# Attention scores in both orders, probabilities written already transposed, and the causal mask as a product in either kind

## The chip, the cores and the metric

One Trainium2 chip, one of its cores. The metric is device time in microseconds from the program's start to its end. TensorE (PE) multiplies, VectorE (DVE) and ScalarE (ACT) empty its banks (PSUM, eight banks of 128 x 512 fp32), GpSimd (POOL) and SyncE (SP) mostly issue transfers here.

## The reference

x is 8 x 512 x 256. Each batch goes through a layer, attention and a feed-forward layer; then a mixture of experts follows for all 4096 tokens.

```python
y = einsum('bnh,boh->bno', x, weight[itok]) + bias[itok]            # layer chosen by batch
Q, K, V = heads(y @ W_Q), heads(y @ W_K), heads(y @ W_V)             # 16 heads of 16
scores = einsum('bhqd,bhkd->bhqk', Q, K) / 4 + causal                # -inf above the diagonal
out = einsum('bhqk,bhkd->bhqd', softmax(scores), V)                  # then reshaped
x = x + out @ W_o
hidden = relu(x @ wi.T + low-rank terms)                             # 1024 wide
h = hidden @ wo.T + low-rank terms
gate = softmax(h @ gate_w + gate_b); top 2 of 8 experts
x = x + sum over the top 2 of gate * expert(h)                       # three layers, gelu
```

## The kernel before, in words

**Stages.** The main stage runs nine rounds (`Round`, b from 0 to 8). Round b computes the attention of batch b and, in the same instruction streams, the feed-forward part of batch b - 1; round 0 has only the first, round 8 only the second. Then come the routing of tokens to experts and 71 tiles of 128 gathered tokens through the experts' three layers. The experts' weights are split into a high and a low part during the rounds: GpSimd loads a piece, ScalarE rounds it (`cast`, L990), GpSimd subtracts (L1516) and writes both to memory (L1521), eight pieces in each attending round.

**Precision.** Most products are of fp32r operands; where more is needed an operand stands as high part plus low part, and a product is three. Transposes and the values times probabilities take fp32.

**One attending round.** `opening` lists the projections q, k, v, the parts of q and k brought into place per pair of heads (`qs`, `ks`, with the constant `sel`), the previous batch's output projection `x1t` and its first hidden tiles. Each head's q and k lie in a strip of 64 rows, its 16 numbers as high and low parts in four groups of 16 rows, so that one product of height 64 gives the score in the precision wanted. Then 35 steps follow (`STEPS`). `units_at(step)` tells for each step:
- two units `s` (a unit is one query tile i of 128 rows and one head; there are 64, sorted by query tile, so that widths are 128, then 256, 384, 512 keys). For each, TensorE adds the causal mask of the last 128 keys as a bf16 product (`mask_b`, `id_b`) and then the score, in a bank of the ring [0, 1, 2]. VectorE takes the negated maximum of each row (L1276), ScalarE the exponential with that as bias per row and with its row sums (L1092), into `probs`;
- two units `t`, one step later: TensorE transposes the 128 x 128 blocks of `probs` (L831, ring [4, 5]); VectorE (L1290) or ScalarE (L1100, `on_act`) copies them to `probs_t`;
- in every second step four units `pv`: values times transposed probabilities, four heads in four groups of 32 columns of the array, fp32, into bank 6;
- at the end of a query tile the reciprocals of the sums (L1301, L1303), their transposes `rt` (L839), and the scaling of the result into `ot_sb` (L1282);
- one piece of filler: the feed-forward of the previous batch or the layer ahead of the next batch (`FILLERS`, ring [3, 7]).

The order on each engine is that of the code; a bank has one semaphore counting its fillings and one counting its emptyings (`filled`, `drained`, `vacant`). A wait on TensorE holds back all that follows it. All products have L665 in the profile (`mm`), and are told apart by their operands.

The lines that the change touches are those of the steps: TensorE's `turn`, ScalarE's `turn` with L1092 and L1100, VectorE's `turn` with L1276, L1290, L1301 and L1303, `psum_plan`, `opening`, and SyncE's loads of the residual (`x_res`) and of the low-rank weights.

## Time and profile before

| what | us |
|---|---|
| median of 3 runs (lowest, highest) | 1510.2 (1505.05, 1514.26) |
| the profiled execution | 1507.66 |
| its span on the core | 1506.1 |
| TensorE busy in the span | 1359.4 |
| weight loads of TensorE (overlap it) | 1053.1 |
| VectorE busy | 875.0 |
| ScalarE busy | 767.0 |
| GpSimd busy | 420.0 |

Mean granted clock of TensorE: 0.955 of full speed. Busy times of pipelined instructions overlap and hold latencies, so the time that one group costs is read from its start to the start of the next. In a row of the timeline, "x2" after a shape means two instructions of the same kind, and the bracket at the end is idle time of the engine before it with what ended it. "2 matmuls" of an fp32 product may be two instructions for one product.

### The profile page before, as it was taken

The numbers are of one execution on the slowest core, as the hardware profiler recorded it, in microseconds if no ns is written. First come the engines' busy times: TensorE is split into PE (matmuls) and PEld (weight loads), VectorE is DVE, ScalarE is ACT, GpSimd is POOL, SyncE is SP. The second block draws the span as 40 slices with busy tenths as digits, with TensorE's granted clock in tenths as the row PEclk, the third lists the DMA queues.
The fourth block names the chain that finished last, engine by engine and source line by source line (L and its number), as shares of the span: only waits on it lengthen the run. The fifth ranks groups of instructions, "written<-read, shape, count | busy, mean of one in ns | idle before, by whom it ended". The sixth has DMA issues, their size and how long they took to land.

```text
span 1506.1 us, 32247 instructions
## 1 busy us (share of the span) xinstructions
PE 1359.4 (90%) x10297; PEld 1053.1 (70%) x10298; DVE 875.0 (58%) x1945; ACT 767.0 (51%) x2003; POOL 420.0 (28%) x553
## 2 busy tenths in 40 slices
PE   5989999999989989999999988249899999999997
PEld 3556766766766766766766757238788888888886
DVE  3765665665665665665666662645455555555554
ACT  4776676665666665675666651013233333333332
POOL 2212211221221211211212210133344444444442
PEclk9799999999999999999999999559999999999999
DMA  6112222222222222222222220652624223342221
GB/s 221 64 66 97 76 82 98 78 96 82 78 95 83 77 81 93 77 86 98 78 80 77 79 72 29 271 225 36 247 42 145 42 42 88 101 148 40 38 40 13
DMA packets 50642, 137.85 MB, mean 92 GB/s; under 512 B 10514, under 2 KB 29586, under 8 KB 48882
## 3 DMA queue, kind: packets, MB, share of 16 engines
q0 software_dynamic: 28992, 68.35, 16.9%
q1 hardware_dynamic: 21554, 68.18, 12.3%
q8 instruction: 65, 1.06, 0.3%
q14 instruction: 31, 0.25, 0.1%
HBM read 86.03 MB, written 51.38 MB: 91 GB/s over the span
## 4 chain that ended last, share of the span: by engine, by line
PE 81%; DVE 5%; ACT 4%; issue 4%; DMA 4%; POOL 1%; SPq 0%; POOLq 0%; DVEq 0%; ACTq 0%
PE bank L665 66%; PE bank L831 9%; PE bank L924 4%; ACT probs L1092 3%; DVE nmax L1276 2%; PE bank L916 1%; DMA xg<-hrows,gid 1%; DMA w_rest<-in_w_all 1%; DMA wsplit<-w_rest 1%; POOL hit_v L1536 0%; PE bank L839 0%; ACT w_high L990 0%; DVE probs_t L1290 0%; POOL w_rest L1516 0%; PE bank L779 0%
## 5 line engine op out<-in xcount | busy, mean ns | idle before, releaser
L1092 ACT ACTIVATE probs<-bank,nmax 128x512 f32<-128x512 f32 (+3 forms) x512 | 266.0, 525 | 164.4 <-DVE nmax L1276 163.0
L1276 DVE TENSOR_REDUCE nmax<-bank 128x1 f32<-128x512 f32 (+3 forms) x512 | 227.3, 486 | 201.7 <-PE bank L665 201.3
L1128 ACT ACTIVATE g<-z 128x512 f32<-128x512 f32 x142 | 89.8, 632 | 281.3 <-DVE z L1466 270.0
L831 PE MATMUL bank<-id_f,probs 128*128 128x128 f32 x1280 | 203.1, 290 | 0.4 <-ACT probs_t L1100 0.4
L1516 POOL TENSOR_TENSOR w_rest<-w_rest,w_high 128x512 f32<-128x512 f32 x64 | 81.4, 1271 | 425.5 <-ACT w_high L990 425.5
L665 PE MATMUL bank<-wst,g1t_high 128*128 x568 | 186.0, 409 | 0.9 <-DVE g1t_low L1454 0.9
L831 PEld LDWEIGHTS bank<-id_f,probs 128*128 128x128 f32 x1280 | 137.8, 143 | 45.0 <-issue 24.2
L1558 POOL DMA_INDIRECT out<-y_sb,sid x71 | 114.3, 1610 | 149.7 <-PE bank L916 67.1
L1290 DVE COPY probs_t<-bank 128x128 f32<-128x128 f32 (+3 forms) x320 | 140.1, 454 | 12.6 <-PE bank L831 12.6
L1466 DVE TENSOR_TENSOR z<-bank,b_sb 128x512 f32<-128x512 f32 x142 | 98.2, 692 | 74.3 <-PE bank L665 63.2
L665 PEld LDWEIGHTS bank<-wst,g1t_high 128*128 128x128 f32 x568 | 102.5, 190 | 20.8 <-issue 1.1
L665 PE MATMUL bank<-wst,g1t_low 128*128 x284 | 113.4, 399 | 0.0
L665 PE MATMUL bank<-wst,g2t_high 128*128 x568 | 107.7, 289 | 1.5 <-DVE g2t_low L1454 1.5
L665 PE MATMUL bank<-k_sb,q_sb 64*128 64x512 f32 (+3 forms) x512 | 107.8, 418 | 0.0
L665 PE MATMUL bank<-mask_b,id_b 128*128 128x128 bf16 x512 | 84.6, 228 | 21.2 <-ACT probs L1092 17.4
L1092 ACT ACTIVATION_READ_ACCUMULATOR probs<-bank,nmax 128x1 f32 x512 | 101.3, 198 | 0.0
L665 PE MATMUL bank<-probs_t,v_sb 128*32 128x128 f32 x2560 | 98.4, 281 | 0.0
L665 PE MATMUL bank<-wst,xgt_high 128*128 x284 | 96.9, 423 | 1.3 <-DVE xgt_low L1454 1.3
L1513 POOL DMA_DIRECT2D w_rest<-in_w_all x64 | 35.0, 546 | 216.4 <-DMA wsplit<-w_rest 216.4
L1548 POOL DMA_INDIRECT xg<-hrows,gid x71 | 76.2, 1073 | 63.8 <-POOL gid L1545 56.8
L665 PEld LDWEIGHTS bank<-probs_t,v_sb 128*32 128x32 f32 x2560 | 62.9, 110 | 41.9 <-issue 28.4
L1100 ACT COPY probs_t<-bank 128x384 f32<-128x384 f32 (+3 forms) x192 | 88.3, 460 | 3.1 <-PE bank L831 2.9
(213 smaller groups left out, 2879.2 us busy)
## 6 DMA issues: line engine op xcount, KB each, us to landing
wst<-wsplit SPq DMA_DIRECT2D x8, 4096.0 KB, 12.6
w_rest<-in_w_all POOLq DMA_DIRECT2D x64, 256.0 KB, 3.1
wsplit<-w_high POOLq DMA_DIRECT2D x64, 256.0 KB, 2.3
wsplit<-w_rest POOLq DMA_DIRECT2D x64, 256.0 KB, 2.6
hrows<-h_sb SPq DMA_DIRECT2D x8, 528.0 KB, 3.0
x_in<-in_xT SPq DMA_DIRECT2D x8, 512.0 KB, 3.5
wb_raw<-in_lora_wb SPq DMA_DIRECT2D x8, 512.0 KB, 3.5
x_res<-in_xT SPq DMA_DIRECT2D x8, 512.0 KB, 4.5
```

Source lines behind the costliest of these rows:

```text
L665: return nc.tensor.matmul(*a, **k)
L831: ins = nc.tensor.transpose(at(n, rd)[:, kb * P:(kb + 1) * P], probs[:, t % 4, kb * P:(kb + 1) * P], id_f[:, :])
L924: ins = nc.tensor.transpose(bank[bt][:, k * P:(k + 1) * P], g[:, k * P:(k + 1) * P], id_f[:, :])
L1092: taken(nc.scalar.activation(probs[:, s % 4, 0:(i + 1) * P], at(n, rd)[:, 0:(i + 1) * P], ACT.Exp, bias=nmax[:, s % 8:s % 8 + 1], accum_ou ...
L1100: taken(nc.scalar.copy(probs_t[:, t % PT_SLOTS, 0:w], at(n, rd)[:, 0:w]), n, rd)
L1128: nc.scalar.activation(g[:, :], z[:, :], ACT.Gelu).then_inc(s_g, 1)
L1276: V.tensor_reduce(nmax[:, s % 8:s % 8 + 1], at(n, rd)[:, 0:(s // HEADS + 1) * P], AX.X, ALU.max, negate=True).then_inc(s_max, 1)
L1290: taken(V.tensor_copy(probs_t[:, t % PT_SLOTS, 0:w], at(n, rd)[:, 0:w]), n, rd)
L1466: V.tensor_tensor(z[:, :], bank[bl][:, :], bias[:, bass.ds(e, 1), :].rearrange("p o n -> p (o n)"), ALU.add).then_inc(s_z, 1)
L1516: nc.gpsimd.tensor_tensor(w_rest[:, :], w_rest[:, :], w_high[:, :].bitcast(F32), ALU.subtract).then_inc(s_wlow, 1)
L1548: nc.gpsimd.indirect_dma_start(xg[:, buffer, :], None, hrows, bass.IndirectOffsetOnAxis(ap=gid[:, 0:1], axis=0), bounds_check=B * S - 1, o ...
L1558: nc.gpsimd.indirect_dma_start(out_rows, bass.IndirectOffsetOnAxis(ap=sid[:, 0:1], axis=0), y_sb[:, buffer, :], None, bounds_check=B * S - ...
```

## The change

- The order of the steps is now by pairs of heads. A pair has three chunks of scores: query tile 3 (512 keys), tiles 2 and 0 in one bank (384 + 128), tile 1 (256). Each chunk takes a bank for either head. They serve only for the row maxima on VectorE (L1276).
- The negated maxima of a pair are split into high and low parts (`m_parts` in `mm_sb`), brought by four products per pair with an identity (`id_r`) into rows `M_ROW`, `M_ROW + 1` of either head's strip, and copied by ScalarE into `q_sb`. k's strip has ones there (`marks_sb[:, 0]`), added when `ks` is emptied; `sel` leaves these rows free.
- Five steps after the first kind, the scores are computed a second time with keys as rows and queries as columns (`st`, ring [4, 5]), with the mask product in the other order; they now hold the maximum's subtraction. ScalarE takes the exponential straight into `probs_t`, without bias and without sums. The transposes, their copies, `probs` and the sums' reads are gone. 64 scores and 64 masks a round become 128 and 128.
- `v_sb` has 16 columns of ones beside each head's 16 of values, so the value product gives the sums too. One group of four heads (`quad`) runs over four key blocks of 512, 384, 256 and 128 columns in one bank: 16 products in place of 40. The result is divided between `ot_sb` and `sums` by masks (`marks_sb[:, 1]`, `[:, 2]`), on ScalarE for even quads and on VectorE for odd ones.
- Twice in a round `sums` is transposed (`nn`, four transposes), its reciprocals are taken and spread (`rrep`), transposed back (`nr`, four) and multiplied into `ot_sb`. Before, the reciprocals were transposed per query tile, two transposes each.
- 34 steps in place of 35, with none, one or two fillers each (`FILL_COUNTS`); `low_o` in four pieces. The residual is loaded into `x1t` in place of `x_res`, after the transposes of x1 are emptied. The low-rank loads wait for the output's transfer as well. GpSimd's part of the stage (split of the experts' weights) stays; its memset fills the ones instead of zeros.

The diff, cut to its core:

```diff
+PAIRS = HEADS // 2
+QUADS = PAIRS // 2
+SCORE_CHUNKS = ((3,), (2, 0), (1,))
+KEY_CHUNKS = ((0,), (3, 1), (2,))
+CHUNKS = len(SCORE_CHUNKS)
+PT_AT = {0: 0, 3: S, 1: S + P, 2: 2 * S}
+PT_COLS = 2 * S + 2 * P
+M_ROW = 32
+MM_COLS = P + 2 * TB
+M_LAG, ST_LAG, PV_LAG, NORM_LAG, SCALE_LAG = 4, 5, 12, 20, 21
+STEPS = NORM_LAG + 2 + 6 * (QUADS - 2)
...
+def work_at(step):
+
+
+    return (chunk_at(step), chunk_at(step - ST_LAG), every(step - M_LAG, CHUNKS, PAIRS),
+            every(step - PV_LAG, 2 * CHUNKS, QUADS), every(step - NORM_LAG, 4 * CHUNKS, KD),
+            every(step - SCALE_LAG, 4 * CHUNKS, KD))
...
+FILL_COUNTS = [2] * 5 + [1] * 7 + [0] + [1] * 5 + [0, 1, 0, 1, 1, 1, 0] + [2] * 5 + [0, 1, 0, 1]
...
-    rings = {"linear": [0, 1, 2, 3, 7, 4, 5, PV_BANK], "score": [0, 1, 2], "filler": [3, 7], "t": [4, 5],
+    rings = {"linear": [4, 5, PV_BANK, 0, 1, 2, 3, 7], "score": [0, 1, 2], "filler": [3, 7], "st": [4, 5],
...
-            probs_t = sb("probs_t", [P, PT_SLOTS, S], F32, attn)
+            v_sb = sb("v_sb", [P, TB, KD, 4, 3, DH], F32, attn)
...
+        def m_parts(part):
+
+            return (mm_sb[:, 0:P].rearrange("p (h c) -> p h c", h=2)[:, :, M_ROW:M_ROW + 2 * TB]
+                    .rearrange("p h (i s) -> p h i s", s=2)[:, :, :, part])
...
-                        pe.wait_ge(free[PV_BANK], rd.start(PV_BANK, 1))
+                        drained(pe, ("nr", KD - 1), Round(p))
...
+                    if score is not None:
+                        g, u = score
+                        if u == 0:
+                            drained(pe, ("qs", g), rd)
+                            drained(pe, ("ks", g), rd)
+                        for half in range(2):
+                            n = ("s", g, u, half)
+                            vacant(pe, n, rd)
+                            for c, (_, cols) in enumerate(query_tiles(u)):
+                                mm(at(n, rd)[:, cols.stop - P:cols.stop], id_b[:, :], mask_b[:, :], start=(c == 0),
+                                   stop=False, skip_group_check=True)
+                    if late is not None:
+                        g, u = late
+                        if u == 0:
+                            drained(pe, ("m", g), rd)
+                        for half in range(2):
+                            n = ("st", g, u, half)
+                            vacant(pe, n, rd)
+                            for c, (_, cols) in enumerate(key_tiles(u)):
+                                mm(at(n, rd)[:, cols.start:cols.start + P], mask_b[:, :], id_b[:, :], start=(c == 0),
+                                   stop=False, skip_group_check=True)
+                    if score is not None:
+                        g, u = score
+                        for c, (i, cols) in enumerate(query_tiles(u)):
+                            for half in range(2):
+                                n, r = ("s", g, u, half), STRIP * half
+                                ins = mm(at(n, rd)[:, cols], q_sb[r:r + STRIP, g, i * P:(i + 1) * P],
+                                         k_sb[r:r + STRIP, g, 0:(i + 1) * P], start=False, stop=True,
+                                         skip_group_check=True)
+                                if c == len(SCORE_CHUNKS[u]) - 1:
+                                    done(ins, n, rd)
+                    if late is not None:
+                        g, u = late
+                        for c, (kb, cols) in enumerate(key_tiles(u)):
+                            for half in range(2):
+                                n, r = ("st", g, u, half), STRIP * half
+                                ins = mm(at(n, rd)[:, cols], k_sb[r:r + STRIP, g, kb * P:(kb + 1) * P],
+                                         q_sb[r:r + STRIP, g, kb * P:S], start=False, stop=True, skip_group_check=True)
+                                if c == len(KEY_CHUNKS[u]) - 1:
+                                    done(ins, n, rd)
+                    if m is not None:
+                        n = ("m", m)
+                        vacant(pe, n, rd)
+                        pe.wait_ge(s_msplit, b * PAIRS + m + 1)
+                        for i in range(TB):
+                            ins = mm(at(n, rd)[:, i * P:(i + 1) * P], mm_sb[:, 2 * i:2 * i + P], id_r[:, :],
+                                     start=True, stop=True)
                         done(ins, n, rd)
-                    if rt is not None:
-                        n = ("rt", rt)
-                        pe.wait_ge(s_rrep, b * TB + (rt + 1))
+                    if norm is not None:
+                        n = ("nn", norm)
+                        vacant(pe, n, rd, [("pv", 2 * norm + 1)])
+                        for i in range(TB):
+                            ins = nc.tensor.transpose(at(n, rd)[:, i * P:(i + 1) * P], sums[:, i * P:(i + 1) * P], id_f[:, :])
+                        done(ins, n, rd)
...
-                        for k in range(KD):
-                            ins = nc.tensor.transpose(at(n, rd)[:, k * P:(k + 1) * P],
-                                                      rrep[:, k * P:(k + 1) * P], id_f[:, :])
+                        pe.wait_ge(s_rrep, b * KD + scale + 1)
+                        for i in range(TB):
+                            ins = nc.tensor.transpose(at(n, rd)[:, i * P:(i + 1) * P], rrep[:, i * P:(i + 1) * P], id_f[:, :])
                         done(ins, n, rd)
-                    if n_fill is not None:
...
-                            done(ins, n, rd)
+                    if quad is not None:
+                        n = ("pv", quad)
+                        vacant(pe, n, rd, [("v", t2) for t2 in range(TB // 2)] if quad == 0 else ())
+                        drained(pe, ("st", 2 * quad + 1, CHUNKS - 1, 1), rd)
+                        for kb in range(TB):
+                            for c in range(4):
+                                h = 4 * quad + c
+                                values = v_sb[:, kb, quad // 2, c, quad % 2:quad % 2 + 2, :]
+                                first = PT_AT[kb]
+                                ins = mm(at(n, rd)[PART * c:PART * (c + 1), kb * P:S],
+                                         values.rearrange("p a d -> p (a d)"),
+                                         probs_t[:, h % PT_SLOTS, first:first + S - kb * P],
+                                         start=(kb == 0), stop=(kb == TB - 1))
+                        done(ins, n, rd)
...
+                    _, late, m, quad, _, _ = work_at(step)
+                    if late is not None:
+                        g, u = late
+                        if u == 0 and g >= 3:
+                            filled(act, ("pv", (g - 3) // 2), rd)
+                        for half in range(2):
+                            n = ("st", g, u, half)
+                            width = key_tiles_width[u]
+                            filled(act, n, rd)
+                            taken(nc.scalar.activation(probs_t[:, (2 * g + half) % PT_SLOTS, S * u:S * u + width],
+                                                       at(n, rd)[:, 0:width], ACT.Exp), n, rd)
+                    if m is not None:
+                        n = ("m", m)
+                        filled(act, n, rd)
+                        for half in range(2):
+                            rows = slice(STRIP * half + M_ROW, STRIP * half + M_ROW + 2)
+                            ins = nc.scalar.copy(q_sb[rows, m, :], at(n, rd)[rows, :])
+                        taken(ins, n, rd)
+                    for n_fill, piece in rd.fillers(step):
+                        take(rd, n_fill, piece)
+                    if quad is not None and quad % 2 == 0:
+                        n = ("pv", quad)
+                        if quad:
+                            filled(act, ("nn", quad // 2 - 1), rd)
+                        filled(act, n, rd)
+                        nc.scalar.activation(ot_sb[:, quad // 2, :], at(n, rd)[:, :], ACT.Identity, scale=marks_sb[:, 1:2])
...
-                    ins = V.tensor_copy((q_sb if what == "qs" else k_sb)[:, m, :], at(n, rd)[:, :])
+                    ins = V.tensor_copy(q_sb[:, m, :], at(n, rd)[:, :])
+                elif what == "ks" and m % 2 == 1:
+                    filled(dve, n, rd)
+                    ins = V.tensor_scalar(k_sb[:, m, :], at(n, rd)[:, :], marks_sb[:, 0:1], None, ALU.add)
...
+                            for i, cols in query_tiles(u):
+                                ins = V.tensor_reduce(nmax[:, g % 2, half, i:i + 1], at(n, rd)[:, cols], AX.X, ALU.max,
+                                                      negate=True)
+                            taken(ins, n, rd)
+                        if u == CHUNKS - 1:
+                            drained(dve, ("s", g, u, 1), rd)
+                            if g > 0:
+                                filled(dve, ("m", g - 1), rd)
+                            V.tensor_copy(m_parts(0), nmax[:, g % 2, :, :]).then_inc(s_mhigh, 1)
+                            dve.wait_ge(s_mhigh, b * PAIRS + g + 1)
+                            V.tensor_tensor(m_parts(1), nmax[:, g % 2, :, :], m_parts(0).bitcast(F32), ALU.subtract
+                                            ).then_inc(s_msplit, 1)
                     if norm is not None:
-                        n = ("pv", norm)
-                        drained(dve, ("rt", norm), rd)
+                        n = ("nn", norm)
...
-            nc.gpsimd.memset(v_sb[:, :, :, :, :].rearrange("p t h a d -> p (t h a d)"), 0.0).then_inc(s_vzero, 1)
+            nc.gpsimd.memset(v_sb[:, :, :, :, 1, :].rearrange("p t k c d -> p (t k c) d"), 1.0).then_inc(s_vzero, 1)
...
         "sel": _np.stack([_np.tile(_np.kron(_np.eye(2), _np.kron(rows, _np.eye(DH))), (4, 1))
-                          for rows in ([[1, 0, 1, 0]], [[0, 1, 0, 1]], [[1, 1, 0, 0]], [[0, 0, 1, 1]])],
+                          for rows in ([[1, 0, 0, 1]], [[0, 1, 0, 0]], [[1, 1, 0, 0]], [[0, 0, 0, 1]])],
                          axis=1).astype(_np.float32),
+        "marks": _np.stack([(iota % STRIP // 2 == M_ROW // 2), (iota % PART < DH), (iota % PART >= DH)],
+                           axis=1).astype(_np.float32),
```

## Rows read from the trace of the kernel before

**Rows 1.** The page: busy times of the span, and the chain that ended last.

```profile
PE 1359.4 (90%) x10297; PEld 1053.1 (70%) x10298; DVE 875.0 (58%) x1945; ACT 767.0 (51%) x2003; POOL 420.0 (28%) x553
...
PE 81%; DVE 5%; ACT 4%; issue 4%; DMA 4%; POOL 1%; SPq 0%; POOLq 0%; DVEq 0%; ACTq 0%
```

**Rows 2.** Table by stretch: four of nine rounds. Bounds, length, busy times, clock, DMA, GB/s.

```profile
17.65:111.77 94.12, 79.50 (x705) 51.37 (x705) 63.66 (x143) 66.78 (x197) 21.75 (x31) 0.85 0.24 85
221.23:331.98 110.75, 103.94 (x921) 75.80 (x921) 70.05 (x161) 71.81 (x204) 23.32 (x32) 1.00 0.26 87
445.06:560.10 115.04, 107.24 (x920) 77.92 (x921) 70.03 (x161) 71.84 (x204) 23.33 (x32) 0.97 0.25 84
891.00:950.00 59.00, 40.35 (x216) 32.63 (x215) 17.82 (x42) 9.00 (x16) 0.00 (x0) 0.85 0.18 64
```

**Rows 3.** Timeline, PE: a round's first mask and the next round's first product. Start, length.

```profile
246.42 0.28 PE L665 MATMUL bank<-mask_b,id_b 128*128 128x128 bf16 x2
...
331.98 0.47 PE L665 MATMUL bank<-cond_high,wq_high 128*128 128x512 f32 x1 [1.56 <-issue]
```

**Rows 4.** Timeline, PE: the groups of one late step of the same round.

```profile
311.18 1.08 PE L665 MATMUL bank<-probs_t,v_sb 128*32 128x128 f32 x32
312.20 0.29 PE L665 MATMUL bank<-mask_b,id_b 128*128 128x128 bf16 x2
312.41 0.50 PE L665 MATMUL bank<-k_sb,q_sb 64*128 64x512 f32 x2
312.84 1.09 PE L831 MATMUL bank<-id_f,probs 128*128 128x128 f32 x8
313.77 0.60 PE L779 MATMUL bank<-id_f,h_sb 128*128 128x128 f32 x4
```

**Rows 5.** Timeline, PE: scores over 128 keys, their transposes, a filler.

```profile
250.53 0.33 PE L665 MATMUL bank<-k_sb,q_sb 64*128 64x128 f32 x2
250.78 0.44 PE L831 MATMUL bank<-id_f,probs 128*128 128x128 f32 x2
250.98 0.48 PE L665 MATMUL bank<-x_high,wi_high 128*128 128x512 f32 x1
...
251.76 0.28 PE L665 MATMUL bank<-mask_b,id_b 128*128 128x128 bf16 x2
```

**Rows 6.** Timeline, PE: the gate's products, reciprocals, next layer.

```profile
326.42 1.85 PE L665 MATMUL bank<-gw_sb,ht_sb 128*128 128x8 f32 x16
328.13 0.41 PE L839 MATMUL bank<-id_f,rrep 128*128 128x128 f32 x2
328.38 1.02 PE L665 MATMUL bank<-x_in,wc_sb 128*128 128x512 f32 x2
```

**Rows 7.** Groups by line, shapes apart: busy us, mean ns, idle before.

```profile
L831 PE MATMUL bank<-id_f,probs 128*128 128x128 f32 x1280 | 203.1, 290 | 0.4 <-ACT probs_t L1100 0.4
...
L1092 ACT ACTIVATE probs<-bank,nmax 128x512 f32<-128x512 f32 x128 | 87.0, 686 | 46.3 <-DVE nmax L1276 46.3
...
L1276 DVE TENSOR_REDUCE nmax<-bank 128x1 f32<-128x512 f32 x128 | 82.4, 686 | 56.9 <-PE bank L665 56.8
...
L1290 DVE COPY probs_t<-bank 128x512 f32<-128x512 f32 x64 | 43.6, 682 | 12.6 <-PE bank L831 12.6
...
L1100 ACT COPY probs_t<-bank 128x512 f32<-128x512 f32 x64 | 37.5, 586 | 3.1 <-PE bank L831 2.9
```

**Rows 8.** Timeline, ACT and PE: a mask that waited for an exponential.

```profile
360.95 0.19 ACT L1092 ACTIVATION_READ_ACCUMULATOR probs<-bank,nmax 128x1 f32 x1
...
361.19 0.23 PE L665 MATMUL bank<-mask_b,id_b 128*128 128x128 bf16 x1 [0.75 <-ACT probs L1092]
```

**Rows 9.** Timeline, ACT and DVE: casts over 32 and 96 rows, a low part.

```profile
325.38 1.04 ACT L1059 CAST wb_top<-wb_raw 32x1024 fp32r<-32x1024 f32 x1
...
327.24 1.04 ACT L1059 CAST wb<-wb_raw 96x1024 fp32r<-96x1024 f32 x1
...
329.06 1.22 DVE L1180 TENSOR_TENSOR wb<-wb_raw,wb_top 32x1024 fp32r<-32x1024 f32 x1
```

More of the change, by code:

```diff
@@ L59 @@
 W_PIECES = W_ALL // W_PIECE
-W_OPENING = (0, 10)
-W_STEPS = (2, 8, 14, 19, 23, 28)
 W_SLOTS = 3
@@ L1076, in turn @@
                     take(rd, n)
-                    if b is not None and rd.opening.index(n) in W_OPENING:
-                        cast(b, W_OPENING.index(rd.opening.index(n)))
+                    if b is not None and n in CASTS_AFTER:
+                        cast(b, CASTS_AFTER[n])
                 for step in range(STEPS):
-                    n_fill, piece = rd.filler(step)
                     if b is None:
-                        if n_fill is not None:
+                        for n_fill, piece in rd.fillers(step):
@@ L1103, in turn @@
+                    if step in CAST_STEPS:
+                        cast(b, CAST_STEPS[step])
                     if step in LORA_STEPS:
@@ L1292, in turn @@
+                    for n_fill, piece in rd.fillers(step - 1) if step > 0 else ():
                         take(rd, n_fill, piece)
```

308 lines of the change are left out of this document (136 added, 172 removed).

## The prediction

> **What bounds the kernel now.** I read the page's shares and the chain first [rows 1]: TensorE is busy for 90% of the span and carries 81% of the chain that ended last, so what counts is the time between the starts of TensorE's groups. Then the table by stage [rows 2]: the attention stage consists of nine rounds, of which eight attend; they lie between 17.65 and 891 us, and the span ends at 1506.1 us, so over 40% of the time (the last round, routing, the experts) is not touched. Then one attending round in order of time, that from 221.23 to 331.98 us: its steps run from the first causal mask at 246.42 to the next round's first matmul at 331.98, which comes after 1.56 us of idle time [rows 3]. That is 85.6 us of steps and 25.2 us of opening. The change leaves the opening's products as they are, so everything happens in the 85.6 us.
>
> **TensorE's attention work before, by start to start.** Two masks take 0.21 us and two scores over 512 keys 0.43 [rows 4]; over 128 keys the two scores take 0.25 [rows 5]. The two scores of a pair use different rows of the array and run side by side, so a pair costs about 0.06 per 128 keys and some 0.20 for starting. A round has 32 pairs, eight of each width: 8 x (0.25 + 0.31 + 0.37 + 0.43) + 32 x 0.21 = 17.6. Transposes: two take 0.20 [rows 5], eight take 0.93 [rows 4]; a round has 16 heads x 10 blocks = 160, eight rounds make the 1280 of the table [rows 7]: 17.4. Values times probabilities: four heads over four key blocks take 1.02 [rows 4]; the 32 instructions are 4 x 0.213 of streaming and 0.17 of start; 40 x 0.213 + 16 x 0.17 = 11.2. Four times two transposes of the reciprocals at 0.25 [rows 6] are 1.0. Together 47.2; the other 38.4 of the 85.6 are the previous batch's feed-forward pieces (I make them 31) and some 7 of stalls.
>
> **After, on TensorE, per round.**
> - Removed: the 160 transposes, -17.4.
> - Scores of both kinds: 128 masks at 0.053 (half of the 0.10 by which two masks exceed one start) are 6.8. The same columns twice are 160 blocks x 0.06 = 9.6. They come in 29 steps, each with one change into masks and one into half-height tiles: 29 x (0.11 + 0.19) = 8.7. The 35 pairs that follow another pair in their step need no new start. No row shows one such pair behind another. Bounds: nothing more than the columns, as between the four key blocks of the value products [rows 4], or the full 0.20 again [rows 5]. I take 0.05, near the value products, since these too change weights every instruction without leaving their tiling: 1.8 (0 to 7). Sum 26.9 against 17.6: +9.3.
> - The maxima as rows: 8 x 4 products of 128 columns. Sixteen weight loads with only eight columns each take 1.71 [rows 6], 0.107 each, so a 128-column product with new weights costs about that: 8 x (0.43 + 0.1) = +4.2.
> - Value products: the same 40 blocks, now 4 starts in place of 16: 9.2, -2.0.
> - Normalisation: 16 transposes in place of 8, in four groups: 2.1, +1.1.
>
> Net -4.8, bounds -7 and +1.
>
> **Stalls.** The transposed scores own two banks, and a step needs both free. So each step is a loop: ScalarE ends its second exponential; 0.05 later TensorE masks (361.19 against the end of the first operation at 361.14 [rows 8]); 0.17 later it scores; ScalarE starts 0.04 after the last pair ends. An exponential over 512 columns costs 0.686 with a pointer bias, a copy without one 0.586 [rows 7]. The new one has no pointer bias, so the copy is the nearer row; I take 0.59, and 1.09 for two overlapping ones.
>
> The Trainium skill (ScalarE: Activation LUTs, What ACT_TABLE_LOAD costs) says that a pointer operand adds about 93 ns to an ACTIVATE. By this rule the new exponential is the cheap one; if it were wrong, each 512-wide step would be 0.2 longer, about 3 us in a round. No row before shows an exponential of that width without bias.
>
> The steps repeat in threes. With 128+384 columns: 0.05 + 0.17 + 0.37 of scores + 0.52 for the last pair + 1.09 = 2.20. With 256: 0.93 to ScalarE, 0.65 for both, and then ScalarE copies the maxima into two rows of q at either half. A cast of 32 rows takes 1.04, as one of 96 does [rows 9], so height doesn't help, and two copies of 512 columns are 1.09; the next step's masks wait for them: 2.74. With 512: 2.02. Three steps are 6.96. TensorE's own work in them is 3.14 + 0.5 of maxima + 3 feed-forward pieces of 0.78 (250.98 to 251.76 [rows 5]) = 6.0, so it idles 1 us in 7. Steps 5 to 23 are six times 6.96, one of 2.0, and two with value products, each 1.2 over its loop: 46.2. Steps 0 to 4 have no transposed scores: scores 3.5, two pieces each 7.4, first maxima 0.5: 11.4. Steps 24 to 33: 3.1, 2.7, 2.3, 2.75, 1.95, 1.4, 2.3, 1.75 (the gate [rows 6]), 1.85 and 0.55; in the 1.85 TensorE waits some 1.3 for VectorE's reciprocals and their spreading. Sum 20.65. Together 78.3, against 85.6 before: -7.3. Of this 4.8 is work and 2.5 stalls, among them the 1.56 [rows 3], since the next batch's projections now end four steps before the round does.
>
> **What is free.** The copies of transposed probabilities leave both engines (0.586 and 0.682 for 512 columns [rows 7]) and the sums' reads leave ScalarE (0.19 [rows 8]), but neither engine was the bound: they gain only slack. It covers the new small work: VectorE per three steps has six maxima (0.686 for 512 columns [rows 7]; 3.6 in all), 0.5 for splitting the maxima and 0.3 of copies, in 7 us. The product of the maxima is issued two steps after they exist; TensorE's wait for it therefore costs nothing, and behind it would stand the step's feed-forward piece. At the round's end the last scale waits on VectorE behind the gate's work and a low part of 1.22 [rows 9]; TensorE meanwhile has the reciprocals' transposes and the first q and k, 3.3, against VectorE's 2.8. If that cover fails, the output projection is late by the difference. The residual, now loaded into the tile where it is added, is requested after step 4 and needed a round later. The expert adapters' loads start after step 26 and are needed 7 us later; the GpSimd chain (casts five or six steps apart, at some 2.3 each, so 12 us) keeps its place. Two key casts gain a pointer bias: 0.1 each, hidden.
>
> **Sum.** Seven rounds x 7 = -49. The first round has no feed-forward pieces: its loops are as long, so -6 by the same count, but it ran at a mean clock of 0.85 [rows 2], and TensorE will be idle for more of it, which I charge 5. So -50 on the profiled execution's 1507.7: 1457.7. The median lies 2.5 above that execution: 1460.
>
> **Rivals.**
> - A, forecast: -4 to -11 per round, 1425 to 1480. Chance 0.55.
> - B, following pairs pay a full start (35 x 0.15 = 5.3): -2 per round, 1495. For it: pairs of 64-row weights have been seen only alone. Chance 0.14.
> - E, loops hide better and TensorE's work alone counts (42 + 31 = 73): -12 per round, 1415. Chance 0.12.
> - D, slower: two banks are too few. The round trip decides once a step of 5 to 23 is 0.38 longer than I count (7.3 / 19), for instance if exponentials don't overlap (0.1 more), ScalarE wakes late (0.2), and the row copies come a further 0.6 late in every third step. At 0.75 longer: +7 per round, 1560 at worst, 1530 in the middle. Against it: the latencies are read from rows. Chance 0.12. The Trainium skill (TensorEngine Tiling (Array Packing), PSUM Bottleneck) warns that tiling speeds up TensorE but not the emptying of PSUM, which may become the bottleneck; this is the mechanism by which it would speak against the change. The trace before does not decide it: its scores had three banks and the transposes two.
> - C, slower by the clock. The round at clock 0.97 took 115.0 us against 110.8 at 1.00 with the same instructions [rows 2]. If the new idle time drew the clock to its lower level (1.2 GHz) for half of steps 5 to 23, their 38 us of TensorE work would double for that half, less the slack: +8 per round, 1570. It decides from about a quarter of the stretch on. Against it: TensorE stays some 85% busy there. Chance 0.07.
>
> Faster by over 0.5% takes A but 0.02, E, and 0.08 of B: 0.73. Within 0.5%: 0.08. Slower: D and C, 0.19. (0.5%, some 7.5 us, is about what a measurement of this kernel can tell from no change.) The range leaves out C, most of D and the lower half of E: 1415 to 1512.
>
> **What would show it.** Right: rounds of about 103 us; no transposes of probabilities; loops of 2.0, 2.2 and 2.7; exponentials at 0.59; idle time before the transposed masks, released by ScalarE; clock near 0.97. Wrong: a following pair over 0.2 (B), idle time over 1 us in every step with ScalarE idle too (D), low clock inside rounds (C).

## The result, and the profile after

| kernel | median us | ratio to before, 95% interval |
|---|---|---|
| before | 1513.2 (5 runs) | 1 |
| after | 1502.4 (5 runs) | 0.9942 (0.9914 to 0.9971) |

The changed kernel is 0.6% faster; its profiled execution took 1502.0 us with a span of 1500.4. The sign was right, the size a fifth of what was forecast: 1460 us with a range up to 1512. The spans differ by 5.7 us, where the forecast had 50.

The page of after: busy times, the clock in 40 slices of the span (9 is 90% or more of full speed), the chain.

```profile
PE 1331.8 (89%) x8825; PEld 999.2 (67%) x8826; DVE 802.8 (54%) x1753; ACT 684.5 (46%) x1301; POOL 418.3 (28%) x553
...
PEclk9569999999999999999999979559999999999998
...
PE 76%; ACT 11%; DVE 7%; DMA 3%; issue 3%; POOL 1%; SPq 0%; POOLq 0%; ACTq 0%; DVEq 0%
```

Against [rows 1], TensorE has 27.6 us less busy time, VectorE 72 and ScalarE 83, and the span hardly moved. TensorE's share of the chain fell from 81% to 76%, ScalarE's rose from 4% to 11%. In the clock row the second and third slice (37 to 112 us) stand out, which are the first round; the one at the 26th and 27th lies behind the attending rounds, and before has it too (its row is 9799..., with one low slice in the first round).

The table by stretch of after: the first and the fourth round (bounds, length, busy times of PE, PEld, DVE, ACT, POOL, clock, DMA share, GB/s).

```profile
17.01:124.78 107.77, 84.86 (x521) 47.74 (x521) 52.91 (x117) 57.30 (x112) 22.88 (x31) 0.71 0.21 81
341.42:450.08 108.66, 100.18 (x739) 69.33 (x737) 60.89 (x136) 61.30 (x116) 23.30 (x32) 0.99 0.25 88
```

The first round grew from 94.1 to 107.8 us, its mean clock fell from 0.85 [rows 2] to 0.71. The six full rounds after it take 108.7 on average ((776.74 - 124.78) / 6), against (785.51 - 111.77) / 6 = 112.3 before. The eighth has no next layer to start; up to the first product of its output projection it grew from 105.0 (890.55 - 785.51) to 108.4 (885.10 - 776.74). TensorE's last groups there, of before:

```profile
890.55 5.33 PE L665 MATMUL bank<-ot_sb,wo_sb 128*128 128x512 f32 x8 [1.46 <-DVE ot_sb L1282]
```

and of after:

```profile
880.48 1.09 PE L891 MATMUL bank<-id_f,sums 128*128 128x128 f32 x4 [1.55 <-DVE sums L1352]
882.58 1.08 PE L898 MATMUL bank<-id_f,rrep 128*128 128x128 f32 x4 [1.01 <-DVE rrep L1379]
885.10 6.25 PE L688 MATMUL bank<-ot_sb,wo_sb 128*128 128x512 f32 x8 [1.43 <-DVE ot_sb L1385]
```

The fourth round of after by stage: opening, steps 0 to 4, 5 to 23, 24 to 33.

```profile
341.42:366.34 24.92, 24.13 (x123) 16.96 (x121) 16.41 (x27) 14.04 (x27) 6.37 (x9) 0.95 0.38 128
366.34:380.63 14.29, 11.96 (x69) 8.32 (x69) 9.60 (x21) 5.24 (x9) 2.37 (x3) 1.00 0.08 33
380.63:427.56 46.93, 44.37 (x389) 31.66 (x386) 28.06 (x73) 28.61 (x57) 9.27 (x13) 1.00 0.24 81
427.56:450.08 22.52, 19.72 (x164) 12.39 (x162) 6.82 (x16) 13.41 (x24) 5.29 (x7) 1.00 0.27 96
```

The forecast for these was 25.2, 11.4, 46.2 and 20.65. The long middle came within 2%; the ends are where the time was lost.

The middle of that round, from ScalarE's and then TensorE's order of time.

```profile
401.29 0.66 ACT L1156 ACTIVATE probs_t<-bank 128x256 f32<-128x256 f32 x2
401.97 1.17 ACT L1163 CAST q_sb<-bank 2x512 fp32r<-2x512 f32 x2
404.11 1.08 ACT L1156 ACTIVATE probs_t<-bank 128x512 f32<-128x512 f32 x2 [0.98 <-PE bank L688]
...
403.19 0.28 PE L688 MATMUL bank<-id_b,mask_b 128*128 128x128 bf16 x2 [0.48 <-ACT q_sb L1163]
403.41 0.39 PE L688 MATMUL bank<-k_sb,q_sb 64*128 64x256 f32 x2
403.63 0.40 PE L688 MATMUL bank<-q_sb,k_sb 64*128 64x512 f32 x2
...
404.91 0.64 PE L688 MATMUL bank<-id_b,mask_b 128*128 128x128 bf16 x4
405.47 0.50 PE L688 MATMUL bank<-k_sb,q_sb 64*128 64x512 f32 x2
405.81 0.45 PE L688 MATMUL bank<-q_sb,k_sb 64*128 64x128 f32 x4
406.19 0.39 PE L688 MATMUL bank<-wf_high,hid_high 128*128 128x256 f32 x1
...
410.21 0.29 PE L688 MATMUL bank<-id_b,mask_b 128*128 128x128 bf16 x2 [0.36 <-ACT q_sb L1163]
```

The loop is what the prediction described. ScalarE's two row copies end at 403.14; the masks of the transposed scores start at 403.19, 0.05 later; scores 0.22 behind them; ScalarE starts at 404.11. Three steps, from 403.19 to 410.21, take 7.02 us; the count was 6.96. The pair of 512 columns of first scores takes 0.34 us and the two pairs of transposed scores behind it (128 and 384 columns) 0.38 together (rows 405.47, 405.81 and 406.19); by the prediction's prices a full start for each would have made it 0.44 and 0.64. So a pair behind a pair needs no full start: rival B is out. Rival D needed steps 0.38 longer than counted; these are 0.02 longer.

Groups of after by line, shapes apart (busy us, mean ns, then idle before them and its releasers).

```profile
L688 PE MATMUL bank<-id_b,mask_b 128*128 128x128 bf16 x512 | 73.0, 228 | 34.7 <-ACT q_sb L1163 26.5 <-ACT probs_t L1156 6.4
...
L1156 ACT ACTIVATE probs_t<-bank 128x512 f32<-128x512 f32 x256 | 139.0, 595 | 113.3 <-PE bank L688 113.3
...
L1163 ACT CAST q_sb<-bank 2x512 fp32r<-2x512 f32 x128 | 73.8, 577 | 8.3 <-PE bank L688 6.3
```

Exponentials of 512 columns are 0.595 us, not 0.686 [rows 7], 0.09 less without the pointer bias. The Trainium skill (ScalarE: Activation LUTs, What ACT_TABLE_LOAD costs) has 93 ns for a pointer operand, and the traces agree: 0.595 us here, 0.684 with the bias put back in `exp_bias`, further down. The copies of two rows cost 0.577 each, as full ones do. TensorE's idle time before the second kind of masks is 34.7 us in all, 26.5 of it for these copies.

The start of the steps in the fourth round, TensorE only.

```profile
366.34 0.22 PE L688 MATMUL bank<-mask_b,id_b 128*128 128x128 bf16 x1
367.83 0.23 PE L688 MATMUL bank<-mask_b,id_b 128*128 128x128 bf16 x1 [1.28 <-DVE hid_low L1287]
...
380.14 0.66 PE L819 MATMUL bank<-id_f,x1t 128*128 128x128 f32 x4 [1.05 <-DVE hid_low L1287]
```

The end of that round and the first products of the next.

```profile
434.69 0.29 PE L688 MATMUL bank<-id_b,mask_b 128*128 128x128 bf16 x2 [1.10 <-ACT q_sb L1163]
...
446.06 1.95 PE L688 MATMUL bank<-gw_sb,ht_sb 128*128 128x8 f32 x16
447.99 0.63 PE L891 MATMUL bank<-id_f,sums 128*128 128x128 f32 x4
449.63 0.80 PE L898 MATMUL bank<-id_f,rrep 128*128 128x128 f32 x4 [1.01 <-DVE rrep L1379]
450.08 0.78 PE L688 MATMUL bank<-cond_high,wq_high 128*128 128x512 f32 x1
450.65 0.63 PE L688 MATMUL bank<-cond_low,wq_high 128*128 128x512 f32 x1
```

Here are three waits that the forecast missed: 1.28 and 1.05 us for VectorE's low part of hidden tiles, and 1.10 for the row copies, which the forecast had in its loops but not as late as here. The fourth, 1.01 for the reciprocals, was in it at 1.3. What was not in it is what follows that one: the first q products start 0.57 and then 0.43 apart (450.08, 450.65), where before they were 0.31 and then 0.23 apart. TensorE is at its lower level, 1.2 GHz (granted clock 0.50 from 450.08 to 453.00), right after a stretch with a wait of 1.01 us, the 16 products of eight columns of the gate, and transposes. Five of the seven round ends in after have such a fall of the clock, all seven have the wait; so the wait alone does not decide it.

### The profile page after: what moved, and what is told of

Same layout as the page of the kernel before. It is cut to its first block, busy times and chain, and to the rows that moved or that the text cites. A ratio compares the mean times of both kernels' runs of the same rounds, so it can differ in the third digit from the quotient of the medians.

```text
span 1500.4 us, 27946 instructions
## 1 busy us (share of the span) xinstructions
PE 1331.8 (89%) x8825; PEld 999.2 (67%) x8826; DVE 802.8 (54%) x1753; ACT 684.5 (46%) x1301; POOL 418.3 (28%) x553
## 4 chain that ended last, share of the span: by engine, by line
PE 76%; ACT 11%; DVE 7%; DMA 3%; issue 3%; POOL 1%; SPq 0%; POOLq 0%; ACTq 0%; DVEq 0%
PE bank L688 69%; PE bank L978 4%; ACT probs_t L1156 4%; ACT q_sb L1163 4%; DVE nmax L1360 2%; PE bank L970 1%; DMA xg<-hrows,gid 1%; ACT ot_sb L1172 1%; DMA w_rest<-in_w_all 1%; PE bank L898 1%; ACT sums L1173 1%; DVE hid_low L1287 1%; DMA wsplit<-w_rest 1%; DVE ot_sb L1350 0%; ACT w_high L1044 0%
## 5 line engine op out<-in xcount | busy, mean ns | idle before, releaser
L1156 ACT ACTIVATE probs_t<-bank 128x512 f32<-128x512 f32 (+1 forms) x384 | 181.1, 524 | 166.7 <-PE bank L688 166.7
L688 PE MATMUL bank<-wst,g2t_high 128*128 x568 | 108.4, 291 | 1.5 <-DVE g2t_low L1544 1.5
L688 PE MATMUL bank<-id_b,mask_b 128*128 128x128 bf16 x512 | 73.0, 228 | 34.7 <-ACT q_sb L1163 26.5
L688 PE MATMUL bank<-k_sb,q_sb 64*128 64x512 f32 (+3 forms) x512 | 93.2, 402 | 0.0
L688 PE MATMUL bank<-mask_b,id_b 128*128 128x128 bf16 x512 | 72.4, 230 | 19.1 <-DVE nmax L1360 9.2
L978 PE MATMUL bank<-id_f,g 128*128 128x128 f32 x568 | 85.8, 274 | 2.4 <-ACT g L1194 2.4
L688 PEld LDWEIGHTS bank<-wst,g2t_high 128*128 128x128 f32 x568 | 86.5, 190 | 1.8 <-issue 1.7
L688 PE MATMUL bank<-q_sb,k_sb 64*128 64x512 f32 (+3 forms) x512 | 82.5, 360 | 0.0
L688 PE MATMUL bank<-probs_t,v_sb 128*32 128x512 f32 (+3 forms) x1024 | 80.6, 458 | 0.0
L688 PE MATMUL bank<-wf_high,hid_high 128*128 128x256 f32 x256 | 80.1, 313 | 0.0
L688 PE MATMUL bank<-wst,g2t_low 128*128 x284 | 79.2, 279 | 0.0
## 6 DMA issues: line engine op xcount, KB each, us to landing
wst<-wsplit SPq DMA_DIRECT2D x8, 4096.0 KB, 12.5
```

The costliest lines, as they stand in the source:

```text
L688: return nc.tensor.matmul(*a, **k)
L978: ins = nc.tensor.transpose(bank[bt][:, k * P:(k + 1) * P], g[:, k * P:(k + 1) * P], id_f[:, :])
L1156: taken(nc.scalar.activation(probs_t[:, (2 * g + half) % PT_SLOTS, S * u:S * u + width], at(n, rd)[:, 0:width], ACT.Exp), n, rd)
```

## Experiments

Each ratio is to the kernel before; after's is 0.9942 with 1502.4 us. The products that some of them add write into a bank whose contents are not read before it is overwritten, so they change only the time. The kernel before was run again beside each group of experiments, with medians of 1509.7 to 1511.7 us against 1513.2 beside after: a difference to after below some 3 us says little.

### first_round_full: the first round's gaps filled

```diff
+                    if p is None and step < 27:
...
+                        for _ in range(3 * FILL_COUNTS[step]):
+                            mm(bank[3][:, :], wq_high[:, 0, 0:P], cond_high[:, 0, :], start=True, stop=True)
```

> The changed kernel, with idle TensorE time of the first round filled: in its steps 0 to 26, three fp32r products of 512 columns into a free bank wherever a later round has a feed-forward piece (their result is overwritten). Nothing else changes, the output stays the reference's. Theory CLOCK: the first round took 107.8 us against 94.1 before because TensorE, with gaps at every step and no feed-forward work, stayed at the lower clock (mean 0.71). With the gaps filled the clock rises early and the first round falls to about 92 us; the whole to 1488. Rival WORK: the round is slow because its chain of ScalarE and VectorE is longer; then it stays at 105 to 110 us or gets longer by the added products, whole 1500 to 1510.

Measured: 1491.8 us, ratio 0.9868 (0.9840 to 0.9896), 10.6 less than after. Its first round, in the table by stretch:

```profile
16.82:112.10 95.28, 85.16 (x611) 53.69 (x611) 52.84 (x117) 57.31 (x112) 22.90 (x31) 0.98 0.25 93
```

95.3 us in place of 107.8, at a clock of 0.98 in place of 0.71, with 90 products more (521 to 611). More work in 12.5 us less time, while VectorE and ScalarE are as busy as in after (52.8 and 57.3 us): the clock is what changed. That the added products cost something at full clock, so that the round stopped at 95 and not at 92, is likely but not shown. Of the 12.5 us the second round gave back 0.8 (108.6 in place of 107.8) and the eighth 1.5 (109.9 in place of 108.4).

### before_first_round_full: the same for the kernel before

```diff
+                        for _ in range(3):
+                            mm(bank[3][:, :], wq_high[:, 0, 0:P], cond_high[:, 0, :], start=True, stop=True)
```

> The kernel before, with the same three products added in steps 0 to 26 of its first round. Theory CLOCK: before had 24 us at the lower clock there, so it gains too, but less: first round from 94.1 to about 88 us, whole 1503 to 1507. Rival WORK: it was already dense, so 3 x 27 products of 0.23 us each (18 us) lengthen it: 100 us or more, whole about 1515.

Measured: 1510.8 us, ratio 0.9994 (0.9978 to 1.0011).

```profile
17.49:113.53 96.04, 89.06 (x786) 59.37 (x786) 63.04 (x143) 67.00 (x197) 21.72 (x31) 0.96 0.24 84
```

The clock rose from 0.85 to 0.96 here too, but the round went from 94.1 to 96.0. Neither theory's number came: the gain of the clock and the cost of 81 products (some 18 us at 0.23 each, partly in gaps) about cancelled. So the remedy paid only after the change, where the gaps are wide; and with the clock up in both (0.98 and 0.96) the first rounds are alike, 95.3 and 96.0, so the change itself is near neutral there.

### m_early: the product of the maxima one step earlier

```diff
-M_LAG, ST_LAG, PV_LAG, NORM_LAG, SCALE_LAG = 4, 5, 12, 20, 21
+M_LAG, ST_LAG, PV_LAG, NORM_LAG, SCALE_LAG = 3, 5, 12, 20, 21
```

> The changed kernel with M_LAG 3 in place of 4: the product of the maxima and ScalarE's two row copies come one step earlier, so that two steps of exponentials lie between the copies and the masks that need them. Theory LOOP: TensorE's wait for the row copies (0.36 to 0.48 us in every third step, 1.1 at step 26) goes, and ScalarE's start of the next exponentials is late by about 0.2 in exchange; each attending round gets 1.5 to 3 us shorter, the whole 12 to 20 us. Rival: TensorE's own work bounds the step, the wait moves to the next pair of masks and the round changes by less than 0.5 us, the whole by less than 4.

Measured: 1483.3 us, ratio 0.9811 (0.9779 to 0.9843), 19.1 less than after. The same group as above:

```profile
L688 PE MATMUL bank<-id_b,mask_b 128*128 128x128 bf16 x512 | 72.1, 229 | 10.8 <-ACT probs_t L1156 8.8
```

The wait for the row copies before these masks (26.5 us) is gone; what is left is 8.8 for exponentials, and some 4.4 for the copies now stands before the first kind of masks. The first round fell from 107.8 to 103.0, the six full ones from 108.7 to 106.5 on average, 2.2 less, as the loop theory has it; its rival (TensorE's work bounds the step) falls. Some of this may be the clock, since only one of the seven round ends now has a fall, but five of the six full rounds have one elsewhere.

### gate_between: the gate between the sums' and the reciprocals' transposes

```diff
-... + [2] * 5 + [0, 1, 0, 1]
+... + [2] * 4 + [1, 0, 1, 1, 1]
```

> The changed kernel with FILL_COUNTS shifted at the end of a round: the last piece of the next layer goes behind the last value product (step 31), the gate behind the transposes of the sums (step 32), so that it lies under VectorE's reciprocals. Theory TAIL: the 1.01 us wait for the spread reciprocals and 0.6 before the next layer's piece shrink, and with less idle time at the round's end the first products of the next round run at the full clock (they started 0.43 apart in place of 0.23, some 1.5 us a round): 2 to 3 us less per full round, 12 to 18 us in all. Rival: the wait is only moved to the transposes of the sums, which wait for VectorE's two operations of 0.74 on the last quad, and the clock falls all the same: under 0.7 us a round, whole within 4 us.

Measured: 1519.7 us, ratio 1.0056 (1.0036 to 1.0076), 17 more than after. Both theories missed. The end of the fourth round, TensorE:

```profile
450.76 0.63 PE L891 MATMUL bank<-id_f,sums 128*128 128x128 f32 x4 [1.23 <-DVE sums L1352]
452.97 3.58 PE L688 MATMUL bank<-gw_sb,ht_sb 128*128 128x8 f32 x16 [1.58 <-DVE cond_low L1254]
456.40 1.09 PE L898 MATMUL bank<-id_f,rrep 128*128 128x128 f32 x4
457.15 0.78 PE L688 MATMUL bank<-cond_high,wq_high 128*128 128x512 f32 x1
```

Two things happened that I had not counted. The transposes of the sums now wait 1.23 us for VectorE's last operation, and the gate 1.58 for `cond_low`, since the gate takes the filler bank in which the next layer's product stands, and VectorE takes that behind its reciprocals. And the clock was down behind the wait (0.50 from 452.97 on): the gate's 16 products took 3.4 us (452.97 to 456.40) in place of 1.9 (446.06 to 447.99). The fourth round became 112.2 us, the six full ones 111.2 on average.

### score_bank: another bank for the second head of step 0

```diff
-    rings = {... "score": [0, 1, 2], ...}
+    rings = {... "score": [2, 0, 1], ...}
```

> The changed kernel with the scores' ring [2, 0, 1] in place of [0, 1, 2]: the second head of step 0 takes bank 0, whose hidden tile is emptied two pieces earlier, not bank 1, where the opening's last hidden tile lies. Theory: the wait of 1.28 us for VectorE's low part at the first mask of a full round goes; a full round gets 1.0 to 1.3 us shorter, the whole 6 to 9 us. Rival: VectorE is behind there anyway, so the wait moves to the next steps (the second transposes of x1 wait 1.05 us for the same queue) and the whole changes by less than 3 us.

Measured: 1489.9 us, ratio 0.9867 (0.9829 to 0.9905), 12.5 less than after, more than expected. The fourth round:

```profile
334.62:440.55 105.93, 98.67 (x739) 68.16 (x738) 60.76 (x137) 61.12 (x116) 23.36 (x32) 1.00 0.27 91
```

The wait of 1.28 us is gone, and five of the full rounds take 105.9 at a clock of 1.00: in those the fall of the clock at the round's start is gone too, which makes up the rest (3.0 us a round for a wait of 1.28). The end of the round is the same as in after:

```profile
438.53 0.63 PE L891 MATMUL bank<-id_f,sums 128*128 128x128 f32 x4
440.17 0.63 PE L898 MATMUL bank<-id_f,rrep 128*128 128x128 f32 x4 [1.02 <-DVE rrep L1379]
440.55 0.48 PE L688 MATMUL bank<-cond_high,wq_high 128*128 128x512 f32 x1
440.88 0.40 PE L688 MATMUL bank<-cond_low,wq_high 128*128 128x512 f32 x1
```

The wait for the reciprocals is still 1.02 us, yet the q products start 0.33 and then 0.23 apart. So what stands right before the fall does not decide it by itself; what else does, whether the wait of 1.28 us earlier in the round or only that the rounds are shorter, was not tested.

### tail_full: products in the gap at the round's end

```diff
+                        if norm == KD - 1:
+                            for _ in range(4):
+                                mm(bank[PV_BANK][:, :], wq_high[:, 0, 0:P], cond_high[:, 0, :], start=True, stop=True)
```

> The changed kernel with four fp32r products of 512 columns (overwritten) between the last transposes of the sums and those of the reciprocals, where TensorE waits 1.01 us for VectorE. Theory CLOCK: without this gap the first products of the next round don't run at the lower clock (0.43 apart, some 1.5 us lost a round): 1 to 1.5 us less per full round, the whole 6 to 9 us less. Rival: the fall comes from the whole end of the round (the gate's 16 short products among it), so the clock falls as before, and the four products cost 0 to 0.3 us a round: whole 0 to 2 us more.

Measured: 1494.0 us, ratio 0.9887 (0.9849 to 0.9925), 8.4 less than after. The end of a round and the next one's start:

```profile
340.54 0.63 PE L901 MATMUL bank<-id_f,rrep 128*128 128x128 f32 x4
340.93 0.48 PE L688 MATMUL bank<-cond_high,wq_high 128*128 128x512 f32 x1
341.25 0.40 PE L688 MATMUL bank<-cond_low,wq_high 128*128 128x512 f32 x1
```

The q products are 0.32 and then 0.23 apart again. Adding four products made this round shorter, 107.3 in place of 108.7, and the six full ones by 1.0 on average (107.7): this fits the clock theory, and its rival (added products cost 0 to 0.3 us) falls. That the products prevent the fall is less sure. At the end of the second round the clock fell in spite of them (the transposes at 231.76 took 1.09 us in place of 0.63), and in `score_bank` and `m_early` most of the same ends keep the full clock without them. A rival that no run tested: any change in the length of a round moves the falls.

### exp_bias: a pointer bias of zeros for the exponential

```diff
-                                                       at(n, rd)[:, 0:width], ACT.Exp), n, rd)
+                                                       at(n, rd)[:, 0:width], ACT.Exp, bias=zero_sb[:, 0:1]), n, rd)
```

> The changed kernel, its exponential given a pointer bias of zeros (one column set by GpSimd at the start). The price of an exponential with pointer bias was 0.686 us at 512 columns, without one 0.59; two overlapping ones 1.28 and 1.09. Theory LOOP: two of three steps are bounded by the round trip over the two banks of transposed scores, so each such step gets 0.1 to 0.2 us longer: 16 steps of 512 columns and 8 of 256, 2 to 4 us a round, the whole 16 to 30 us more. Rival WORK: TensorE's own work bounds the steps; ScalarE has slack, and the whole changes by less than 5 us.

Measured: 1527.0 us, ratio 1.0115 (1.0075 to 1.0156), 24.6 more than after.

```profile
L1157 ACT ACTIVATE probs_t<-bank,zero_sb 128x512 f32<-128x512 f32 x256 | 161.9, 684 | 112.9 <-PE bank L689 112.2
```

0.684 in place of 0.595 us, and 24.6 us over eight rounds, 3.1 a round: the round trip over the two banks carries the step, although ScalarE is idle for over two fifths of the stage. The rival, under 5 us, falls. With the bias left in, the change would have been slower than before.

### three: m_early, score_bank and first_round_full together

> The changed kernel with three edits together: M_LAG 3, the scores' ring [2, 0, 1], and the first round's gaps filled. If they act on separate places: m_early gave 19 us, the filled first round 11 us (less of M_LAG's share in the first round, some 4), the ring 6 to 9: 1502 - 19 - 8 - 7 = 1468, 1463 to 1475. Rival: what one gives back the next wait takes, 1480 or more.

Measured: 1458.5 us, ratio 0.9651 (0.9607 to 0.9694). Opening, steps 0 to 4, 5 to 23 and 24 to 33 of the fifth round:

```profile
426.72:450.35 23.63, 22.85 (x123) 15.99 (x122) 16.46 (x28) 13.83 (x27) 5.84 (x8) 1.00 0.37 123
450.35:463.73 13.38, 11.86 (x70) 8.25 (x70) 9.50 (x21) 5.24 (x9) 2.94 (x4) 1.00 0.16 59
463.73:508.07 44.34, 43.38 (x389) 31.47 (x387) 27.88 (x73) 28.52 (x57) 9.46 (x13) 1.00 0.24 78
508.07:529.86 21.79, 19.90 (x164) 12.44 (x162) 6.75 (x16) 13.42 (x24) 5.30 (x7) 1.00 0.33 111
```

This round, and two more like it, take 103.1 us, where the forecast had 103.5 for the changed kernel; the six full ones take 104.3 on average, since the clock still falls in the other three. The first round takes 94.0. The sum of the three single gains over after is 10.6 + 19.1 + 12.5 = 42.2; together they gave 43.9, more than expected (1463 to 1475), mostly since the ring had been put at 6 to 9. Within what the runs can tell, the gains add up; the rival falls.

### three_tail and all: towards the best version

`three_tail` adds the four products of `tail_full`. `all` adds further:

```diff
-FILL_COUNTS = [2] * 5 + [1] * 7 + ...
+FILL_COUNTS = [2] * 4 + [1, 2] + [1] * 6 + ...
...
+                    if p is not None and not rd.leads and step in (31, 32, 33):
+                        for _ in range(6):
+                            mm(bank[4][:, :], wq_high[:, 0, 0:P], cond_high[:, 0, :], start=True, stop=True)
```

> The three edits and the four added products at the end of a round. The clock still fell near some round starts with the three edits, and the wait of 1.02 us for the reciprocals is still there. Theory CLOCK: 0.5 to 1.5 us less a full round, 1450 to 1455. Rival: the falls are gone already with the shorter rounds, so nothing is left to gain: within 2 us of 1458.

Measured: 1456.0 us, ratio 0.9642 (0.9618 to 0.9666), 2.5 less than `three`, which the intervals don't tell from nothing, and less than the clock theory had. In `three` only three of the six full rounds had a fall left, and in `three_tail` three still have one, two of them some 39 us after the round's start, where the added products can't help.

> As three_tail, and two more: the second transposes of x1 go to step 5 (FILL_COUNTS 2, 2, 2, 2, 1, 2, 1 ...), since they wait 1.52 us for VectorE's low part in a full round; and in the eighth round, which has no next layer, six products of 512 columns (overwritten) in each of the last three steps, where TensorE waits 2.3, 1.0 and 1.4 us and the clock falls. Theory: the x1 wait falls under the scores of step 5, 0.8 to 1.2 us less a full round, and the end of the eighth round 3 to 5 us less: 1438 to 1446. Rival: VectorE's low part is itself late, so the wait only changes its place, and the added products delay the chain that ends the round: 1449 or more.

Measured: 1444.5 us, ratio 0.9564 (0.9543 to 0.9585), 4.4% faster than before and 3.8% faster than after. Its fourth round, from the first added product of one end to that of the next:

```profile
316.04:418.24 102.20, 98.97 (x744) 68.78 (x742) 60.49 (x136) 60.88 (x117) 23.46 (x32) 1.00 0.28 94
```

The transposes of x1 wait 2.4 us in all in place of 10.6 in `three_tail`. The eighth round's first q product and its output projection (TensorE in order of time):

```profile
726.49 0.48 PE L688 MATMUL bank<-cond_high,wq_high 128*128 128x512 f32 x1
...
830.61 3.60 PE L688 MATMUL bank<-ot_sb,wo_sb 128*128 128x512 f32 x8
```

That is 104.1 us in place of 108.4 in after and 105.7 in `three_tail`, at a clock of 1.00 in place of 0.97. So the earlier step for x1 and the 18 products gave the eighth round 1.6 us together, where the products alone had been put at 3 to 5; the full rounds took 102.2 in place of at least 103.1, 0.9 less, as expected for x1.

## Why the prediction was wrong

The forecast had -50 us on the span, the trace -5.7. The steady loop was priced rightly. What failed are the charge for the first round's clock, the waits at the start and the end of a round that the forecast took as free, and the clock of the full rounds. By its own terms:

- **TensorE's work and the loops, steps 5 to 23: right.** 46.9 against 46.2 us; three steps 7.02 against 6.96; the price of following pairs, exponentials and copies as taken. Rivals B and E are out: a full start per pair isn't paid, and the loops bind (`exp_bias`, `m_early`).
- **"The first round ... which I charge 5": this term was mis-sized.** It should be 20: the round was forecast 1 us shorter and became 13.7 longer. This is rival C's mechanism, which I had dismissed with TensorE's 85% in full rounds and priced only there. In the first round there are no feed-forward pieces, and I had the loops' length (seven) and TensorE's own work in them (3.6) at hand: half idle. `first_round_full` gives 12.5 of it back by adding work that raises the clock; `m_early` gives back 4.8 by a shorter loop, at a clock still of 0.73.
- **"Steps 0 to 4 ... 11.4": 14.3.** I read the change of the `linear` ring as free, "the opening's products as they are". It moves the opening's last hidden tiles from banks 3 and 7 into banks 0 and 1, which step 0's scores need; VectorE's low part of the last one ends 1.28 us late. `score_bank` undoes this alone, and gave 12.5 us in all. The second wait, 1.05 before x1's transposes, is behind VectorE's four maxima in the same queue: "VectorE was not the bound" is true of its load and not of its order.
- **Steps 24 to 33, 20.65: 22.5.** Step 25, put at 2.7, took 3.8: ScalarE comes to its exponentials and row copies only behind the two operations on the quad's result and a cast (432.27), so the masks of step 26 wait 1.10. And 0.6 for `cond_low` was missing.
- **The clock of full rounds: not priced.** I took the 110.8 us round as the base; before's six average 112.3, and I took no fall of the clock for after. Five of its rounds start at the lower level or just before it (0.95 in the opening of the fourth); a full round with such a fall takes 108.7 to 108.9, and one without takes 107.3 to 107.4 in `tail_full`, so a fall costs some 1.5 us. The kernel before falls at another place: its first q products are 0.23 us apart, but the opening of its fourth round (the table by stretch, below) is at 0.93, the fall lying after 346 us. So it isn't the change alone that costs clock; it moves it.

```profile
331.98:357.00 25.02, 22.41 (x112) 15.71 (x113) 13.09 (x24) 11.90 (x23) 5.81 (x8) 0.93 0.40 138
```

- **The eighth round** was forecast 7 us shorter and became 3.3 longer. Its end has no next round's products to fill it, and there the new order has three waits in a row, 4.0 us together (1.55 for the sums, 1.01 for the reciprocals, 1.43 for the scaled output), where before waited 1.46 for the last alone; TensorE's transposes between them run at the lower level (1.09 us for four, 0.63 at 447.99). No run tested this alone: with four products in the second wait it took 108.6 (`tail_full`), and `all` at full clock 104.1 against 105.7, with another edit beside it. How much of the 10 is the clock and how much the waits stays open.

Of the 44 us that failed to come, 14.7 belong to the first round, 20 to the six full ones (108.7 against 112.3 each, where 7 had been forecast), and 10 to the eighth; 0.6 came back ahead of the first round, which starts earlier. By stage, the fourth round is 5.2 over its forecast of 103.45: 2.9 in steps 0 to 4, 1.9 in steps 24 to 33, 0.7 in the middle, -0.3 in the opening. What follows the first output product is equal: 615.3 us after (1500.4 - 885.10), 615.6 before (1506.1 - 890.55).

The time lies inside the range of 1415 to 1512, near its slow end, and 0.6% faster is just beyond what I called no change, to which I gave 0.08. No case of mine led there: rivals B to E each priced one mechanism in the full rounds, and what happened was a sum of small ones at the ends of rounds and a large one in the first. That the time is inside the range, and its sign right, is luck: the range was wide enough for B and part of D, which did not happen.

## What to carry to other kernels

When a change takes work off the engine that bounds, look for the stretch where nothing fills the hole: there its clock may fall, and harmless products can then be faster than none, as in the first round here. When a plan of banks or an order is rotated, price the waits of the first and last few steps one by one; the steady loop is the easy part. In a loop over two banks, try a late step's by-product a step ahead: here one lag was worth 19 us, where the whole change had brought 11.

## What the runs showed of the hardware

- Added TensorE work shortened a round: 90 products more, 107.8 to 95.3 us, with the granted clock from 0.71 to 0.98. In the kernel before, 81 more were neutral (94.1 to 96.0), at 0.85 to 0.96.
- The same end of a round, with 16 products of eight columns, transposes and a wait of 1.0 us, had a fall to 1.2 GHz for the next products (0.43 in place of 0.23 us for 512 columns) in five of seven cases in after, but in two of seven in `score_bank` and one of seven in `m_early`, whose rounds differ elsewhere. With four products of 512 columns in that wait it was one of seven (`tail_full`). The gate's 16 products of eight columns ran at the lower level when two waits came before them (3.4 us in place of 1.9).
- A pointer bias costs an exponential 0.09 us (0.684 against 0.595 at 512 columns).
- A copy of two rows of 512 costs ScalarE as much as one of 128 rows (0.577 against 0.586).
- Pairs of products of half height, one behind another with new weights, take 0.34 us for 512 columns and 0.38 for 128 + 384 up to the next kind of product, with nothing like the 0.20 of a start for each (rows 405.47 to 406.19 of after).
